# Where the loop's body begins on each engine of a two-layer graph attention kernel: TensorE's border moved from in front of the scores to in front of the output and v products

## The reference

```python
def _L0(x, adj):                       # layer 0
    q, k, v = x @ Wq.T, x @ Wk.T, x @ Wv.T + bv        # split into 12 heads
    scores = einsum(q, k) * 384**-0.5 + 2 * adj        # adj serves as both encodings
    scores = where(any(scores != 0, -1), scores, -inf)
    return nan_to_num(softmax(scores)) @ v @ Wo.T + bo
def _L1(x, adj):                       # layer 1
    q, k, v = x @ Wq + bq, x @ Wk + bk, x @ Wv + bv
    scores = einsum(q, k) / sqrt(32) + beta * adj
    return softmax(where(adj > 0, scores, -9e15)) @ v
x = layernorm(x + _L0(x, adj)); x = layernorm(x + _L1(x, adj))
```

## Time and profile before

| | |
|---|---|
| median of 3 runs | 2124.54 us (2122.32 to 2125.64) |
| the profiled execution, its own time | 2125.58 us |
| its span, first to last instruction | 2123.8 us |
| TensorE matmuls | 2046.2 us busy, 96% of the span |
| TensorE weight loads | 1923.4 us, 91% |
| ScalarE | 1888.1 us, 89% |
| VectorE | 1814.6 us, 85% |
| GpSimd | 1643.1 us, 77% |
| granted TensorE clock, mean | 0.985 |

### The profile page before, as it was taken

How to read it: one execution, slowest core, us unless ns; L and a number is a source line. 1 busy time by engine, 2 the same in 40 slices (tenths; PEclk the granted TensorE clock), 3 DMA queues, 4 the chain that set the end, 5 groups by cost and what they waited for, 6 DMA issues and landing times.

```text
span 2123.8 us, 86803 instructions
## 1 busy us (share of the span) xinstructions
PE 2046.2 (96%) x23808; PEld 1923.4 (91%) x23808; DVE 1814.6 (85%) x8324; ACT 1888.1 (89%) x7816; POOL 1643.1 (77%) x2187
## 2 busy tenths in 40 slices
PE   5799999999999999999999999999999999999984
PEld 5799999999999999999999999999999999999973
DVE  3578888888988988888988988988989888888875
ACT  4489999999999999999999999999999999999975
POOL 2667877888877878878878888888888888787774
PEclk9899999999999999999999999999999999999997
DMA  4245555555555555555555555555555555555554
GB/s 134 58 101 136 135 130 136 132 128 135 132 136 127 133 139 124 136 135 128 138 134 130 137 133 130 141 131 126 139 132 129 134 132 136 127 132 139 118 122 107
DMA packets 225439, 274.19 MB, mean 129 GB/s; under 512 B 25681, under 2 KB 225361, under 8 KB 225361
## 3 DMA queue, kind: packets, MB, share of 16 engines
q1 hardware_dynamic: 225360, 273.26, 53.5%
HBM read 46.67 MB, written 25.17 MB: 34 GB/s over the span
## 4 chain that ended last, share of the span: by engine, by line
PE 87%; POOL 4%; issue 3%; DMA 3%; SPq 2%; DVE 1%; ACT 0%; POOLq 0%; DVEq 0%
PE r_bank L356 22%; PE r_bank L357 21%; PE r_bank L358 21%; PE s_bank L407 10%; PE r_bank L423 8%; DMA prob0T<-flip 2%; PE r_bank L339 2%; PE r_bank L349 2%; PE r_bank L435 2%; SPq L291 1%; POOL prob L924 1%; POOL flip L897 1%; DVE flip L711 1%; POOL w_lo L845 0%; DMA stage<-in_L_gnn_Wv_dram 0%
## 5 line engine op out<-in xcount | busy, mean ns | idle before, releaser
L586 ACT ACTIVATE prob<-neg_s,heads 128x128 f32<-128x128 f32 x3072 | 1191.1, 394 | 18.7 <-DVE flip L711 11.1
L586 ACT ACTIVATION_READ_ACCUMULATOR prob<-neg_s,heads 128x1 f32 x3072 | 594.2, 193 | 0.0
L924 POOL TENSOR_TENSOR prob<-prob,heads 128x512 f32<-128x512 f32 x384 | 389.2, 1042 | 98.7 <-DVE heads L783 98.7
L897 POOL TENSOR_TENSOR flip<-neg_s 128x768 f32<-128x768 f32 x128 | 235.8, 1842 | 186.6 <-DMA prob0T<-flip 171.3
L356 PE MATMUL r_bank<-xT_hi,w_hi 128*128 128x256 f32 x1152 | 357.9, 311 | 14.6 <-DVE xT_lo L717 13.6
L695 DVE CUSTOM_DVE_ANT_0 neg_s<-s_bank,bias 128x128 f32<-128x128 f32 x1536 | 333.5, 286 | 20.6 <-PE s_bank L407 18.9
L695 DVE CUSTOM_DVE_ANT_0 neg_s<-s_bank,adj 128x128 f32<-128x128 f32 x1536 | 333.8, 286 | 2.3 <-PE s_bank L407 1.6
L356 PE MATMUL r_bank<-x1T_hi,w_hi 128*128 128x256 f32 x1152 | 330.8, 287 | 3.8 <-DVE x1T_lo L717 3.8
L358 PE MATMUL r_bank<-xT_hi,w_lo 128*128 128x256 f32 x1152 | 327.9, 285 | 0.0
L357 PE MATMUL r_bank<-xT_lo,w_hi 128*128 128x256 f32 x1152 | 327.9, 285 | 0.0
L357 PE MATMUL r_bank<-x1T_lo,w_hi 128*128 128x256 f32 x1152 | 325.0, 282 | 0.0
(11 more groups left out here) (85 smaller groups left out, 5493.6 us busy)
## 6 DMA issues: line engine op xcount, KB each, us to landing
prob0T<-flip SPq DMA_DIRECT2D x512, 192.0 KB, 3.6
prob1T<-stage SPq DMA_DIRECT2D x512, 192.0 KB, 3.6
x_in<-in_x_dram SPq DMA_DIRECT2D x128, 192.0 KB, 3.3
out_dram<-y SPq DMA_DIRECT2D x128, 192.0 KB, 2.3
adj<-in_adj_dram SPq DMA_DIRECT2D x256, 64.0 KB, 2.7
prob<-in_L_gnn_Wq_dram SPq DMA_DIRECT2D x1, 576.0 KB, 5.6
prob0T<-in_L_gnn_Wk_dram SPq DMA_DIRECT2D x1, 576.0 KB, 6.5
stage<-in_L_gnn_Wv_dram SPq DMA_DIRECT2D x1, 576.0 KB, 7.6
```

The costliest lines, as they stand in the source:

```text
L586: act.activation(prob[layer][:, h, :], neg_s[layer][:, h, :], ACT.Exp, bias=neg_max[layer][:, h:h + 1], scale=-1.0, accum_out=row_sum[laye ...
L897: pool.tensor_tensor(fold_a, neg_s[0][:, :, 0:N // 2], neg_s[0][:, :, N // 2:N], ALU.add).then_inc(fold_steps, 1)
L924: pool.tensor_tensor(prob[0][:, hs, :], prob[0][:, hs, :], inv_sum0[:, hs].unsqueeze(2).to_broadcast([P, HC, N]), ALU.mult).then_inc(probn ...
```

## The change

The list of steps is rotated, engine by engine: steps from the end of body n-1 become the first of body n, or the first of body n+1 become the last of body n. The order in which each engine takes its steps stays as it was, with one exception noted below; what moves is the place where the loop's turn begins and ends, and so also which steps lie in front of the loop and behind it.

- TensorE: the 13 steps from `project_out0(m1,1)` to `attend(1,m3,0)` go to the front, for a pair one lower. The border lies in front of `project_out0`.
- ScalarE: the first 19 steps, `out1T_out(m4,0)` to `exps(1,m3,1,0,2)`, go to the end, for a pair one higher. The border lies in front of `exps(0,n,0,10,12)`.
- VectorE: the nine steps `flip_probs(1,m3,1)` to `low_xT(p2,0)` go to the front. The border lies in front of `flip_probs(1,m4,1)`.
- GpSimd: `late_x1` goes from the front to the end; the border lies behind it.
- The exception: ScalarE's `high_weights(WQ1, WK1, WV1)` in the bodies ahead of the loop now comes behind the 19 moved steps of pair -1 and in front of the rest of that body, where it stood behind the rest.

```diff
@@ TensorE body
+                project_out0(m2, 1, r)
+                project_v(0, n, 0, r)
+                project_v(1, m3, 0, r)
+                scores(1, m3, 0, r)
+                project_qk(0, n, 4, r)
+                project_v(1, m3, 1, r)
+                project_v(0, n, 1, r)
+                transpose_x1(m2, 0, r)
+                project_qk(0, n, 5, r)
+                transpose_x1(m2, 1, r)
+                transpose_x(p1, 0, r)
+                attend(0, m1, 0, r)
+                attend(1, m4, 0, r)
                 scores(0, n, 0, r)
...
                 transpose_out1(m4, 1, r)
-                project_out0(m1, 1, r)
...
-                attend(1, m3, 0, r)
@@ ScalarE body
-                out1T_out(m4, 0)
-                exps(1, m3, 0, 2, 4)
...
-                exps(0, n, 0, 8, 10)
-                exps(1, m3, 1, 0, 2)
                 exps(0, n, 0, 10, 12)
...
                 high_o0T(n, 0)
-                if is_peeled(r, off, -1):
+                out1T_out(m3, 0)
+                exps(1, m2, 0, 2, 4)
...
+                exps(0, p1, 0, 8, 10)
+                exps(1, m2, 1, 0, 2)
+                if is_peeled(r, off, -2):
                     high_weights(WQ1, WK1, WV1)
@@ VectorE body
+                flip_probs(1, m4, 1)
+                inverse_sums1(m4, 1)
+                values_out0(n, 0)
+                negate(1, m3, 0, (0, 1, 2, 3))
+                values_out0(n, 1)
+                low_x1T(m2, 0)
+                abs_max(m1, 1)
+                inverse_sums0(m1, 1)
+                low_xT(p1, 0)
                 low_x1T(m2, 1)
...
                 attention_out1(m4, 1)
-                flip_probs(1, m3, 1)
...
-                low_xT(p2, 0)
@@ GpSimd body
-                late_x1(m3, 0)
                 make_bias1(m3, 1)
...
                 normalise0(n, 1)
+                late_x1(m2, 0)
```

More of the change, by code:

```diff
@@ L453, in body @@
                 n = Pair(r, off)
-                m4, m3, m2, m1, p1, p2 = (n.plus(-4), n.plus(-3), n.plus(-2), n.plus(-1), n.plus(1), n.plus(2))
+                m4, m3, m2, m1, p1 = (n.plus(-4), n.plus(-3), n.plus(-2), n.plus(-1), n.plus(1))
+                project_out0(m2, 1, r)
[11 more added lines that the diff above has]
+                attend(1, m4, 0, r)
                 scores(0, n, 0, r)
@@ L592, in body @@
                 n = Pair(r, off)
-                m5, m4, m3, m2, m1, p1, p2 = (n.plus(-5), n.plus(-4), n.plus(-3), n.plus(-2), n.plus(-1), n.plus(1), n.plus(2))
-                out1T_out(m4, 0)
-                exps(1, m3, 0, 2, 4)
-                high_xT(p1, 1)
-                if is_peeled(r, off, -1):
[L599 to L612, removed]
-                exps(0, n, 0, 8, 10)
-                exps(1, m3, 1, 0, 2)
+                m4, m3, m2, m1, p1, p2 = (n.plus(-4), n.plus(-3), n.plus(-2), n.plus(-1), n.plus(1), n.plus(2))
                 exps(0, n, 0, 10, 12)
@@ L639, in body @@
                 high_o0T(n, 0)
-                if is_peeled(r, off, -1):
+                out1T_out(m3, 0)
+                exps(1, m2, 0, 2, 4)
+                high_xT(p2, 1)
+                if is_peeled(r, off, -2):
+                    high_weights(WO0)
+                qk_out(1, m1, 0, r)
+                exps(1, m2, 0, 4, 6)
+                qk_out(1, m1, 1, r)
+                exps(1, m2, 0, 6, 8)
+                qk_out(0, p2, 0, r)
+                exps(1, m2, 0, 8, 10)
+                exps(0, p1, 0, 0, 2)
+                exps(1, m2, 0, 10, 12)
+                qk_out(1, m1, 2, r)
+                exps(0, p1, 0, 2, 8)
+                qk_out(1, m1, 3, r)
+                norm_apply1(m4, 1)
+                qk_out(1, m1, 4, r)
+                exps(0, p1, 0, 8, 10)
+                exps(1, m2, 1, 0, 2)
+                if is_peeled(r, off, -2):
                     high_weights(WQ1, WK1, WV1)
@@ L792, in body @@
                 n = Pair(r, off)
-                m5, m4, m3, m2, m1, p1, p2 = (n.plus(-5), n.plus(-4), n.plus(-3), n.plus(-2), n.plus(-1), n.plus(1), n.plus(2))
+                m5, m4, m3, m2, m1, p1 = (n.plus(-5), n.plus(-4), n.plus(-3), n.plus(-2), n.plus(-1), n.plus(1))
+                flip_probs(1, m4, 1)
[7 more added lines that the diff above has]
+                low_xT(p1, 0)
                 low_x1T(m2, 1)
```

## The result

The changed kernel takes 2222.36 us in the median (2217.49 to 2226.94, 6 runs), the kernel before 2122.45 us (2120.98 to 2125.64, 6 runs): ratio 1.0468, 95% interval 1.0452 to 1.0484. So it is 100 us slower; the forecast was 34 us slower, with a range that ended at 2190. The profiled execution has a span of 2225.1 us.

A forecast was written before the change was run, and what follows sets the result against it. TensorE was taken to bound the kernel (87% of the chain). VectorE's late fetches, 39.8 us, less TensorE's 6.2 gave +33.6 us: 2159.2 on the profiled execution, median 2158; 80% range 2116 to 2190.

The forecast's parts named there:

- TensorE, -6.2 us: Scores behind TensorE's old loop border: moving it saves 0.24 us in each of 26 taken branches, 6.2 us.
- The store of four pieces: VectorE's and ScalarE's instruction stores hold four 128-record pieces; the moved loops reach a fifth, so every piece is fetched again.
- Rival A: The store holds a fifth piece or the loop's top is asked for early enough: only 6.2 us count, 2118.3; chance 0.31.
- The price of the missing piece: VectorE's border: fetch asked for on entering the fifth piece takes 2.7 us; `flip_probs` 2.5 us late, TensorE waits 1.53 us.
- The bound of 4.2 us: Upper bound using GpSimd's fetch time for VectorE's missing piece: 4.0 us late, 3.0 us of TensorE wait, 2196 us.
- the term of 39.8: TensorE's waits for late VectorE results at the loop border: 26 x 1.53 = 39.8 us.
- ScalarE, 0 us: ScalarE's moved border costs nothing: its queue is 2.1 us ahead, and 34 records in a fifth piece cover the fetch.
- Rival C: ScalarE's 16 records behind the jump are too few; 1 us more each turn, 2184; 0.12 together with the upper bound.
- TensorE's code: TensorE's loop code spans eight 256-record pieces instead of seven; whether they fit was unknown, cost put at nothing.
- weight roundings: Three roundings of 1.16 us ahead of the loop come some 9 us earlier: taken as 0, bounds -1 and +2 us.
- GpSimd: One addition moved past GpSimd's loop border, between operations of 1 us: costs nothing.
- Rival B: The 0.24 us don't go away, or moved borders eat small reserves elsewhere: within 4 us of before, 2124; chance 0.07.

The follow-up runs named there:

- 77: The changed kernel with VectorE's loop laid 77 records behind the start of a piece, so the turn ends on the fourth piece's last record: 2117.45 us.
- 78: The changed kernel with VectorE's loop laid 78 records behind the start of a piece, one record (the branch) in a fifth piece: 2223.38 us.

## Why the prediction was wrong

The direction was right, and so was the chain of causes up to one step: when the loop's top is asked for. The size was off by a factor of three. By its own steps:

- TensorE, -6.2 us: right. Its border alone gave -7.6 us (-9.3 to -4.7 by the interval), a turn shorter by 0.23 us.
- The store of four pieces, and that the border moves the code onto a fifth: right, and exact to one record (77 against 78). Rival A, that a fifth piece is held or is asked for early enough, falls for this kernel; its second half is true with 34 records (2120 us).
- The price of the missing piece, the step that failed: "The loop's top is asked for on entering the fifth piece", and from it "with 2.7 the jump is over at 1094.0 ... 2.5 us late". With the six records that the sum counted, it holds (2.26 us late, 2152 us). The changed kernel has four, because its turn is two records shorter than the one whose length I took over from the trace of before. With one, four or five the packet starts 1.9 us behind the branch in place of 0.6 and the hint runs 3.7 us behind it: `flip_probs` is 3.52 us late, TensorE waits 2.82 in place of 1.53. I had treated six records and four as the same case; nothing in the trace of before told them apart. Turn against turn, both from branch to branch at full clock: 65.99 against 64.35 with six records ((2003.1 - 329.9) / 26), 26 x 1.64 = 43 us.
- The clock, a term that the sum lacked: 27.5 us. With waits of 2.5 to 3.0 us TensorE's clock fell in 17 of 26 turns; with 1.0 to 1.4 us (six records) it is 1.00 over the whole loop. The bound of 4.2 us gave 4.0 us late, 3.0 of wait and 2196, which misses the measured time by about this term (26 us). That its lateness was near is luck: the 4.2 us were another engine's, and on VectorE it is 1.8 us from packet to hint wherever the packet came late.
- In sum: the term of 39.8 is 74.1 + 6.2 = 80.3 for lateness, and 27.5 for the clock; 107.8 - 6.2 = 101.6, the difference of the profiled executions within 0.3 us.
- ScalarE, 0 us: right in size, wrong in its reason. I counted 34 records in a fifth piece and some five packets a turn. The changed kernel has only VectorE's packets (122; with VectorE's border alone 120), five a turn and not ten. Line 103 shows that its loop was entered by something longer than the next instruction: MOVE at 289.1, hint at 290.1; before it took 0.1 us (277.3 and 277.4). I read that as a head that was laid on the next edge, so that 433 records fit. The first turn bears it out: besides VectorE's (275.6, 295.9 and 316.5 us, at its records 47, 175 and 303) it has small packets at 291.4, 310.4 and 330.4 us, each 1.2 to 2.0 us behind ScalarE's records 0, 128 and 256 (290.1, 309.2, 328.4); with a head 112 records into a piece they would have to follow its records 16, 144 and 272 (291.7, 312.0, 331.1), and all three start before those. No run tried this by itself, but 32 records in a fifth, set by hand, cost nothing either. The DMA views of 291.2 to 291.6, 310.2 to 310.6 and 330.3 to 330.7 us:

```profile
q14 instruction: 1, 0.01, 4.8%
...
q14 instruction: 1, 0.01, 8.6%
...
q14 instruction: 1, 0.01, 6.8%
```

- Rival C falls for the change; with a single record it would have come to 13 us.
- TensorE's code, weight roundings, GpSimd: nothing, as predicted. The eight pieces that I feared fit.
- Rival B falls: 7.6 us came back.

Open: why the packet starts later with five records than with six on VectorE, and whether their number or their time decides; why ScalarE with one record is at 2.2 us; and why the fall of the clock skips every second or third turn. Nothing here tells.

The best of these versions is the change without VectorE's part, or with its loop laid so that it fits: 2115.85 and 2117.16 us, no different from TensorE's border alone (2116.07).

## What to carry to other kernels

Moving a border moves the loop's code behind it, and an engine's loop that fills its store almost to the last record can go over by any edit in front of it or in it: count records from the edge, with the new turn's own length, and lay the loop's head by hand where they don't fit. Instruction packets inside a loop are the sign, but not the price: look when the first packet of a border starts, before the branch or behind it. When a sum gives TensorE a new standstill of some 3 us in each turn, add what its clock may lose behind it.

## What had not been expected of the hardware

- VectorE's store: 512 records fit, 513 don't, and the one record costs 106 us in 26 turns (2117.45 and 2223.38 us).
- A loop over five pieces fetches five a turn and may still cost 0 to 3 us if enough records lie in the fifth (32 on ScalarE, 2116.2 us; 34 on VectorE, 2120.03 us).
- From branch to hint on VectorE: 0.3 us or less with the top in the store, 0.5 with 34 records in the fifth piece, 2.1 and 2.4 us with six, 3.7 with one, four or five; on ScalarE 2.2 with one. The packet starts 4.7 us ahead of the branch with 34 records, 0.4 to 0.6 us behind it with six and 1.9 us behind it with one, four or five.
- The granted clock at 0.51 for 3.4 us behind standstills of 2.5 to 3.0 us in 17 of 26 turns, 1.6 us each; in three of 26 with standstills of 1.2 to 1.7 us (2162.76 us); in none with standstills of 1.0 to 1.4 us (2152.08 us).
